# One PSUM tensor for the ring, and one read for a quad of banks: exponentials and row maxima of an attention block on one Trainium2 core

## The reference

```python
mod = (silu(c) @ wmod)                            # six vectors per sequence: sa, ca, ga, sb, cb, gb
h = layernorm(x) * (1 + ca) + sa
q, k, v = projections(h)                          # 16 heads; 16 content and 64 rotary columns each
attn = softmax(q @ k.T / sqrt(80) + causal mask)  # 512 x 512 per head
x = x + ga * (attn @ v) @ w_out.T
h = layernorm(x) * (1 + cb) + sb
x = x + gb * ffn(h)                               # 32 experts routed, top 8, merged to 8 groups: gate, up, down
```

## The kernel before, in words

| PE step (banks) | latest reader it waits for |
|---|---|
| score.000 (1-4) | maxima.010 (3-6), heads 0, 1 |
| maxima.011 (6,0,1,2) | score.000 (1-4), heads 0, 1 |
| score.001 (4,5,6,0) | maxima.011 (6,0,1,2), heads 0, 1 |
| maxima.012 (2-5) | score.001 (4,5,6,0), heads 0, 1 |
| score.002 (6,0,1,2) | maxima.012 (2-5), head 0 |
| score.011 (5,6,0,1) | score.010 (0-3), heads 0, 1 |
| score.012 (0-3) | maxima.020 (3-6), head 0 |
| maxima.021 (5,6,0,1) | score.012 (0-3), heads 0, 1 |
| score.020 (1-4) | maxima.030 (4,5,6,0), head 0 |
| score.021 (5,6,0,1) | score.020 (1-4), head 0 |
| maxima.032 (0-3) | maxima.031 (3-6), head 0 |
| score.022 (4,5,6,0) | maxima.032 (0-3), head 0 |
| score.031 (1-4) | score.030 (3-6), heads 0, 1 |
| score.032 (5,6,0,1) | score.031 (1-4), head 0 |
| maxima.101 (0-3) | maxima.100 (3-6), head 0 |

## Time and profile before

### The profile page before, as it was taken

One profiled execution on the slowest core, in us unless ns is written; L12 is line 12 of the kernel. 1 busy time (PEld: TensorE's weight loads), 2 busy tenths in 40 slices (PEclk: granted clock), 3 DMA queues, 4 the chain that ended last, 5 costly groups with the idle time before them and its releaser, 6 DMA issues.

```text
span 1099.2 us, 24746 instructions
## 1 busy us (share of the span) xinstructions
PE 1016.1 (92%) x9744; PEld 723.9 (66%) x9744; DVE 770.1 (70%) x1516; ACT 401.3 (37%) x723; POOL 412.8 (38%) x349
## 2 busy tenths in 40 slices
PE   6979989999899989999899998999999998999678
PEld 4546667766676667766677666766677766776456
DVE  6767687585957868677785859678686777857344
ACT  4335433254314443145331543144431453314310
POOL 1526342264505353154422635054430544326100
PEclk9989989999999999999999999999999999999969
DMA  6220000200002000200002000020002000010000
GB/s 190 58 88 2 3 1 1 68 2 2 1 4 66 2 1 1 69 2 2 1 1 69 2 2 1 2 69 2 1 1 68 2 2 1 1 49 2 2 1 20
DMA packets 22233, 23.59 MB, mean 21 GB/s; under 512 B 6315, under 2 KB 20139, under 8 KB 22131
## 3 DMA queue, kind: packets, MB, share of 16 engines
q1 hardware_dynamic: 22130, 22.02, 6.6%
HBM read 17.80 MB, written 4.21 MB: 20 GB/s over the span
## 4 chain that ended last, share of the span: by engine, by line
PE 78%; DVE 7%; issue 7%; POOL 4%; ACT 2%; DMA 1%; DVEq 0%; POOLq 0%; SPq 0%; ACTq 0%
PE ring L1124 17%; PE ring L981 12%; PE ring L982 10%; PE ring L983 10%; PE ring L1196 8%; PE av L1140 6%; PE ring L1104 6%; PE ring L1095 2%; DVE mcol L863 2%; PE ring L1112 1%; PE ring L1185 1%; PE ring L1042 1%; ACT pt L672 1%; POOL rows L553 1%; POOL prod L547 1%
## 5 line engine op out<-in xcount | busy, mean ns | idle before, releaser
L672 ACT ACTIVATE pt<-ring 128x384 f32<-128x384 f32 (+1 forms) x384 | 170.8, 531 | 329.6 <-PE ring L1124 293.4
L562 POOL TENSOR_SCALAR_AFFINE_SELECT pt<-pt 128x512 f32<-128x512 f32 x128 | 79.7, 638 | 413.1 <-ACT pt L672 413.1
L863 DVE TENSOR_REDUCE mcol<-ring 128x1 f32<-128x128 f32 (+3 forms) x512 | 212.2, 481 | 19.3 <-PE ring L1104 17.8
L839 DVE TENSOR_TENSOR prod<-ring,table 128x1024 f32<-128x1024 f32 x128 | 155.3, 1217 | 97.7 <-PE ring L983 97.0
L1124 PE MATMUL ring<-rows 32*128 32x512 f32 (+3 forms) x3072 | 165.4, 329 | 18.4 <-ACT pt L672 8.5
L553 POOL TENSOR_TENSOR rows<-prod,rows 128x1024 fp32r<-128x1024 f32 x64 | 152.6, 2394 | 36.7 <-ACT rows L652 36.7
L1124 PEld LDWEIGHTS ring<-rows 32*128 32x128 f32 x3072 | 120.0, 185 | 69.4 <-issue 33.1
L546 POOL TENSOR_TENSOR prod<-prod 128x512 f32<-128x512 f32 x64 | 82.6, 1290 | 134.8 <-DVE prod L839 134.4
L652 ACT ACTIVATE rows<-prod 128x1024 fp32r<-128x1024 f32 x64 | 67.1, 1061 | 60.3 <-PE ring L1124 39.3
L1140 PE MATMUL av<-pt,vals 128*17 128x512 f32 (+3 forms) x1024 | 84.7, 436 | 3.3 <-POOL pt L562 3.2
L1196 PE MATMUL ring<-dn,pt 128*128 128x256 f32 x384 | 85.0, 381 | 0.0
(11 more groups left out here) (162 smaller groups left out, 1609.2 us busy)
## 6 DMA issues: line engine op xcount, KB each, us to landing
xn<-x_dram SPq DMA_DIRECT2D x8, 512.0 KB, 4.0
xr<-x_dram SPq DMA_DIRECT2D x8, 512.0 KB, 3.7
out_dram<-xr SPq DMA_DIRECT2D x8, 512.0 KB, 3.2
gate_bc<-gates_scratch SPq DMA_DIRECT2D x8, 256.0 KB, 4.9
pt<-wmod_dram SPq DMA_DIRECT2D x1, 1536.0 KB, 6.5
pt<-gup_t_dram SPq DMA_DIRECT2D x16, 96.0 KB, 2.6
dn<-wu_t_dram SPq DMA_DIRECT2D x1, 640.0 KB, 10.1
xr<-wk_t_dram SPq DMA_DIRECT2D x1, 512.0 KB, 8.2
```

The lines of the kernel that those rows point to most:

```text
L672: sc.activation(pt[:, PT_AT[n] + h * w:PT_AT[n] + (h + 1) * w], ps[:, 0:w], ACT.Exp, scale=SCALE).then_inc(exp_ready.sem, 1)
L839: ve.tensor_tensor(prod[:, s % PROD, :, :], ps[:, :].unsqueeze(1).broadcast_to([P, 2, S]), table[:, :, :], ALU.mult).then_inc(rotated.sem, 1)
L863: last = ve.reduce_max(mcol[:, q, h * HR + HD:h * HR + HD + 1], ps[:, at:at + (q + 1) * P], AX_X)
```

## The change

The seven tensors `ring0` to `ring6` become one tensor `ring` of seven banks. `bank` hands out the same banks as before. A new helper `runs` cuts a quad into its runs of neighbouring banks: one run of four, or two where the quad passes from bank 6 to bank 0. ACT now takes the exponential of a whole run in one instruction, and DVE the row maxima of a whole run in one instruction (in the third maxima job one for each of the two row blocks). The semaphore goes up by the number of heads in the run, when the instruction is complete.

```diff
-        ring = [ctx.enter_context(nc.psum_tensor(f"ring{i}", [P, 512], F32)) for i in range(RING)]
+        ring = ctx.enter_context(nc.psum_tensor("ring", [P, RING, 512], F32))
...
         def bank(part, place):
-            return ring[(place if part == "setup" else NSETUP + place) % RING]
+            return ring[:, (place if part == "setup" else NSETUP + place) % RING, :]
+
+        def runs(part, step):
+
+            at = [(PLACES[part][0][(*step, h)] + (0 if part == "setup" else NSETUP)) % RING for h in range(HG)]
+            wrap = next((h for h in range(1, HG) if at[h] < at[h - 1]), HG)
+            return [(h0, n, ring[:, at[h0]:at[h0] + n, :]) for h0, n in ((0, wrap), (wrap, HG - wrap)) if n]
...
                         wait_full(sc, b, part, ("score", ahead, g, n, HG - 1))
-                        for h in range(HG):
-                            ps = bank(part, PLACES[part][0][("score", ahead, g, n, h)])
-                            sc.activation(pt[:, PT_AT[n] + h * w:PT_AT[n] + (h + 1) * w], ps[:, 0:w], ACT.Exp,
-                                          scale=SCALE).then_inc(exp_ready.sem, 1)
+                        for h, many, banks in runs(part, ("score", ahead, g, n)):
+                            sc.activation(pt[:, PT_AT[n] + h * w:PT_AT[n] + (h + many) * w].rearrange("p (h q) -> p h q", q=w),
+                                          banks[:, :, 0:w], ACT.Exp, scale=SCALE).then_inc(exp_ready.sem, many)
...
                         wait_full(ve, b, part, ("maxima", ahead, g, i, HG - 1))
-                        for h in range(HG):
-                            ps = bank(part, PLACES[part][0][("maxima", ahead, g, i, h)])
+                        for h, many, banks in runs(part, ("maxima", ahead, g, i)):
                             for q, at in MAX_JOBS[i]:
-                                last = ve.reduce_max(mcol[:, q, h * HR + HD:h * HR + HD + 1], ps[:, at:at + (q + 1) * P], AX_X)
-                            last.then_inc(max_read.sem, 1)
+                                own = mcol[:, q, :].rearrange("p (h r) -> p h r", r=HR)[:, h:h + many, HD]
+                                last = ve.reduce_max(own, banks[:, :, at:at + (q + 1) * P], AX_X)
+                            last.then_inc(max_read.sem, many)
```

## The result

| | before | after |
|---|---|---|
| median of the runs, us | 1102.49 (1101.96 to 1103.27) | 1216.96 (1214.33 to 1218.38) |
| profiled execution, us (span) | 1101.17 (1099.2) | 1217.06 (1215.2) |
| mean granted clock | 0.98 | 0.965 |

The changed kernel is slower: ratio 1.104 (1.102 to 1.106), 114.5 us. The forecast was 1213 (1185 to 1242).

What follows compares the result with a forecast made beforehand. PE, busy 92% of the span, was taken to bound the kernel. Span 1099.2 + 100 for late releases + 11 for the clock = 1210.2, with 2.0 around it and 1.3 to the median: 1213 us (1185 to 1242).

Steps and rivals of the forecast that it cites:

- Lengths of merged reads: On ACT and DVE, a merged read takes its columns plus one tail: four banks of 512 in 1.90 and 2.30 us.
- The lower bound: Merged read length with the steps between banks gone: 1.90 us on ACT, 2.30 on DVE for four of 512.
- the old step: Upper bound for merged reads: 489 (ACT) and 599 ns (DVE) a bank kept inside, 20 us more in the whole program.
- What is removed: Beside a busy PE: 13.7 us of ACT and 21.4 of DVE, priced at 0 to -3 us, taken as -1.
- The fourteen places: Starts of PE in a pass that wait for banks freed late by merged reads: 13.0 us in a pass.
- They add up: Late starts of PE sum, since a late PE delays the next read: seven body passes x 13.0 = 91 us.
- Last pass and set-up: Late releases outside the body passes: 9 us (7 to 11) in the last pass, 0 (to 1.4) in set-up.
- The clock: Falls of PE's clock behind maxima.101, 3 us, and from score.020 to score.022, 8 us: 11 taken, bounds 0 to 34.
- (1): Rival: PE catches up, 2.5 us of each pass absorbed, no added clock fall: about 1187 us; chance 13%.
- (2): Rival: the clock falls again and again in the attention part, four times a pass: say 1248 us; chance 14%.
- (3): Rival: PE waits for a quad's last bank, not the first, so merging is faster: 1074 us; chance 3%.
- (4): Rival: release not lengthened, count rising within an instruction or reads far faster: within 2 us of 1102; chance 2%.

Runs made afterwards that it cites:

- unwanted_only: The changed kernel, but quads whose head 0 or 1 PE wants soon (15 in a body pass) read bank by bank: 1103.89 us, ratio 1.0002 to before.
- the single quads: Two kernels, each merging one quad of each pass in the kernel before: maxima.020 1122.70 us, ratio 1.0191; score.020 1130.58 us, ratio 1.0258.

## Why the prediction was right, step by step

- *Lengths of merged reads.* Forecast 1.90, 1.47 and 1.14 us on ACT, 2.30 and 1.76 (1.76 for three banks of 512 too) on DVE, 1.82 for the third job; measured 1.88, 1.45, 1.13, 2.29, 1.755, 1.758 and 1.82. The lower bound was right, the old step isn't kept inside an instruction.
- *What is removed.* ACT 15.9 us and DVE 23.1 less busy, forecast 14 and 21. The Trainium skill (Perfetto Trace Analysis, section Optimizing Scalar/DVE Operations) gives 51 ns of overhead for a ScalarE instruction and 125 for a DVE one on PSUM; the busy times give 15.9 / 241 = 66 and 23.1 / 357 = 65 ns, so for DVE the page's figure is twice what this kernel shows. Its advice to break instructions up where an engine isn't saturated but causes bubbles elsewhere is borne out: the kernel before and `unwanted_only`, both at 1103 us, against the changed one.
- *The fourteen places.* Lateness of PE that each adds, mean over the body passes, forecast and measured: score.000 0.88, 1.21; maxima.011 0.70, 0.67; score.001 0.60, 0.49; score.002 0.48, 0.44; score.011 0.73, 0.71; score.012 1.61, 1.64; maxima.021 0.25, 0.25 (but 1.0 and 1.2 in two passes, at the low clock); score.020 1.07, 1.10; score.021 1.26, 1.37; maxima.032 1.15, 1.10; score.022 1.24, 1.19; score.031 0.63, 0.62; score.032 0.77, 0.78; maxima.101 1.65, 1.67. maxima.012 escaped, as it should. Only score.000 is clearly mis-sized, and its 0.33 us in seven passes are 2 us.
- *They add up.* 13.0 us in a pass were forecast, the measured ones sum to 13.2, and PE's waits for reads came to 125.7 us (forecast some 125). maxima.101 started 600.64 - 598.29 = 2.35 us after the read of maxima.100 began (forecast 2.4).
- *Last pass and set-up.* The down product of the last pass came 11.6 us later relative to the one before it: 10.4 at the places (forecast 9, 7 to 11) and 1.2 in a fall of the clock behind score.020; the set-up lost 0.7 us (0 to 1.4).
- *The clock.* I took 11 us: 3 behind maxima.101 and 8 from score.020 to score.022. The lateness that belongs to no release, with what before lost in its own falls taken off, is 1.7 us a pass in the loop, 11.6 in the seven body passes and 1.2 in the last, together nearly 13. It sits where it was expected. The clock falls behind maxima.101 in all seven body passes, which is 1.0 us more in each of the three passes of the loop that had no fall there before. It falls behind score.021 in six of the seven; in two, one of them the pass without that fall, it falls behind maxima.021. The stretch from score.021 to maxima.032 is 1.5 us longer for it, where I had priced a fall at 1.05. With bounds of 0 and 34 us this term was a choice, and that it came out is in part luck: the single quads show that it doesn't follow the length of one gap.
- *Rivals.* Nothing was absorbed (1), the clock fell twice in a pass of the loop and not four times (2), all fourteen places came later, where a PE that waited for the last bank would have started 0.2 us sooner (3), and the count did not go up within an instruction (4).

The sum over the starts of the down products: six body passes took 771.0 us and take 860.8, 89.7 more (15.0 each, of which 13.3 are the releases and 1.7 the clock); the first pass took 14.0 more, the last 11.6, the set-up 0.7. That is 116.0, which is what the span has grown by (1215.2 - 1099.2). The forecast for the span was 111: 100 for the places and 11 for the clock, where some 103 and 13 were measured.

## What to carry to other kernels

A read over several banks frees the first of them when the last is read. Where a bounding engine wants the first bank, that costs it the rest of the read, however idle the reader is; merge reads only where nobody waits for their first banks. Where the reader doesn't set the time, that brings nothing either; a kernel in which it does was not tried here. Look behind each new gap of the bounding engine at the granted clock, since that can cost more than the gap. And in a ring a step that is moved takes its place with it, so the steps seven places on have to be looked at again.

## What the runs showed of the hardware

- One ACT or DVE instruction reads four PSUM banks at the rate of one bank: 1880 ns for 4 x 512 columns, 2292 ns for the maximum, and the semaphore goes up by four at its end (PE 0.06 to 0.14 us later).
- What a gap costs through the clock isn't proportional to it. 1.34 us more at score.021 made the clock fall there, and for 6.8 us behind maxima.101, where the gap was unchanged (1.54 us); with all quads merged the gap at maxima.101 was 3.20 us and half clock lasted only 3.4. Which history of PE decides it stays open.
- Matmuls that are overwritten keep the clock up: 0.72 became 1.00, and nine of them in two gaps of a pass took 1.04 us off a pass that had the fall (129.09 to 128.05).
- The saving of instructions on engines that PE doesn't wait for is real and doesn't show in the time: 16.5 us of busy time in `unwanted_only`, no change of the time.
